# Eight tiles in flight instead of six in the experts phase, with the steps of four engines reordered

## The reference, cut to what matters

```python
def _L0_ffn_ref(x, Wg, W1, W2):
    cap = max(1, T // E)                        # T = 8192 tokens, E = 8 experts
    probs = jax.nn.softmax(xt @ Wg, axis=-1)
    _, top_idx = jax.lax.top_k(probs.T, cap)    # every expert picks its tokens
    ...
    tok2exp = jnp.where(assigned, jnp.argmax(masked, axis=0), jnp.argmax(pT, axis=0))
    weights = jnp.take_along_axis(probs, tok2exp[:, None], axis=1)[:, 0]
    for e in range(E):
        gate = jnp.where(tok2exp == e, weights, 0.0)
        h = jax.nn.gelu(xt @ W1[e], approximate=False) @ W2[e]
        out = out + gate[:, None] * h

xn = _layernorm(x)
s = _L0_attn_ref(xn, ...)                       # the RWKV block
g = _silu(_L0_ffn_ref(xn, Wg, W1, W2))
x = x + s * g
```

## Time and profile before

| | us |
|---|---|
| median of 3 runs | 1236.12 |
| the profiled execution, its own time | 1236.41 |
| its span, first to last instruction | 1234.6 |

### The profile page before, as it was taken

How to read it: one execution, slowest core, us unless ns; L and a number is a source line. 1 busy time by engine, 2 the same in 40 slices (tenths; PEclk the granted TensorE clock), 3 DMA queues, 4 the chain that set the end, 5 groups by cost and what they waited for, 6 DMA issues and landing times. The chain is left out here.

```text
span 1234.6 us, 20795 instructions
## 1 busy us (share of the span) xinstructions
PE 1052.4 (85%) x5440; PEld 836.5 (68%) x5441; DVE 905.4 (73%) x1997; ACT 681.1 (55%) x1233; POOL 371.2 (30%) x403
## 2 busy tenths in 40 slices
PE   5589999999999999999888898998877777777775
PEld 5367877677767767777666676677766666666665
DVE  5899789898898888898986878645555555555554
ACT  2646648568568568567363855744443444433443
POOL 4031321010010010001025537441544454444452
PEclk9789999999999999999988999999999999999999
DMA  9423221011011010010101105351222222222210
GB/s 303 140 86 102 69 85 35 0 53 51 0 51 48 3 51 29 22 51 9 43 14 39 52 1 171 103 185 35 87 66 74 69 70 76 68 72 67 66 50 10
DMA packets 60055, 80.46 MB, mean 65 GB/s; under 512 B 7774, under 2 KB 47327, under 8 KB 60002
## 3 DMA queue, kind: packets, MB, share of 16 engines
q1 hardware_dynamic: 48658, 54.69, 14.0%
q0 software_dynamic: 11360, 25.32, 6.9%
HBM read 65.17 MB, written 26.49 MB: 74 GB/s over the span
## 5 line engine op out<-in xcount | busy, mean ns | idle before, releaser
L916 PE MATMUL psKV<-arena 128*128 128x256 f32 x1024 | 236.1, 385 | 3.4 <-ACT arena L619 1.7
L916 PEld LDWEIGHTS psKV<-arena 128*128 128x128 f32 x1024 | 193.9, 193 | 42.6 <-issue 14.8
L988 PE MATMUL psM<-arena 128*128 128x128 f32 x1152 | 147.1, 281 | 54.6 <-ACT arena L716 48.7
L988 PEld LDWEIGHTS psM<-arena 128*128 128x128 f32 x1152 | 135.7, 193 | 68.8 <-issue 68.8
L709 ACT ACTIVATE arena<-arena,info_t 128x256 f32<-128x256 f32 x72 | 43.1, 600 | 207.5 <-DVE info_t L1486 192.5
L426 POOL TENSOR_SCALAR lnw<-mv 128x4 f32<-128x4 f32 x32 | 8.8, 275 | 485.3 <-DVE mv L1308 485.1
L1557 DVE TENSOR_TENSOR hT_rounded<-arena,hT_rounded 128x512 fp32r<-128x512 f32 x72 | 49.9, 693 | 132.8 <-ACT hT_rounded L728 132.8
L486 POOL DMA_INDIRECT out_dram<-arena,out_idx x72 | 73.2, 1016 | 168.0 <-DVE row_idx L1481 152.1
L1327 DVE SCALAR_TENSOR_TENSOR arena<-arena,vecs 128x512 f32<-128x512 f32 x160 | 108.7, 746 | 0.0
L473 POOL DMA_INDIRECT arena<-xs_rows,row_idx x66 | 100.3, 1519 | 23.1 <-issue 23.1
L886 PE MATMUL psM<-mix_hi,wfk_hi 128*128 128x512 f32 x256 | 103.6, 405 | 2.5 <-ACT mix_hi L608 1.3
(11 more groups left out here) (208 smaller groups left out, 2413.8 us busy)
## 6 DMA issues: line engine op xcount, KB each, us to landing
desk<-in_x SPq DMA_DIRECT2D x16, 512.0 KB, 5.1
arena<-in_x SPq DMA_DIRECT2D x16, 512.0 KB, 4.0
desk<-in_xT SPq DMA_DIRECT2D x16, 512.0 KB, 4.1
xs_rows<-s_ring SPq DMA_DIRECT2D x16, 512.0 KB, 3.2
xs_rows<-in_x SPq DMA_DIRECT2D x16, 512.0 KB, 4.6
desk<-in_W SPq DMA_DIRECT2D x8, 512.0 KB, 8.5
arena<-in_W SPq DMA_DIRECT2D x8, 512.0 KB, 7.5
out_dram<-arena,out_idx POOLq DMA_INDIRECT x72, 2.5
```

The lines of the kernel that those rows point to most:

```text
L916: ins = pe.matmul(psKV[:, j // 2, (j % 2) * C:(j % 2 + 1) * C], kf2[:, h, j * P:(j + 1) * P], wfv[:, h, :], start=(h == 0), stop=(h == HC ...
L988: ins = pe.matmul(psM[:, i % 2, f * P:(f + 1) * P], w1_t[i % 2][:, k, f * P:(f + 1) * P], xnT[i % 2][:, k, :], start=(k == 0), stop=(k == ...
```

## The change

RING goes from 6 to 8, so there are eight buffers for rows and for results, and the steps are written out as 8, 7 passes of 8, and 8. The end of the area for these buffers (`moe_end`) moves behind two more tiles of the first phase. The order inside the steps becomes:

- PE: `mlp_in(t+1)`, `mlp_out(t)`, `turn_x(t+3)`
- ACT: `gelu(t+1)`, `tanh(t)`, `take_xn(t+3)`, `xn(t+4)`
- DVE: `combine(t)`, `take_index(t+8)`, `take_info(t+8)`, `split_h(t+2)`, `mlp_input(t+4)`

What comes ahead of the first step is filled up to match: one `turn_x`, one `take_xn`, one `xn`, one `split_h` and one `mlp_input` more, and eight infos taken at once instead of three.

```diff
-RING = 6
+RING = 8
-        moe_end = at[0]
         mixB_r = part(CH * SEQ)...
         kf2 = part(HC * SEQ)...
+        moe_end = at[0]
...   (ACT)
             def step(t, i, g):
-                if not isinstance(t, int) or t < NT - 3:
-                    xn(t + 3, (i + 3) % RING, g + (i + 3) // RING)
                 if not isinstance(t, int) or t < NT - 1:
                     gelu(t + 1, (i + 1) % RING)
-                if not isinstance(t, int) or t < NT - 2:
-                    take_xn(t + 2, (i + 2) % RING)
                 tanh(t, i)
+                if not isinstance(t, int) or t < NT - 3:
+                    take_xn(t + 3, (i + 3) % RING)
+                if not isinstance(t, int) or t < NT - 4:
+                    xn(t + 4, (i + 4) % RING, g + (i + 4) // RING)
...   (ahead of the steps)
             xn(2, 2, 0)
+            xn(3, 3, 0)
             gelu(0, 0)
+            take_xn(2, 2)
...   (PE)
             def step(t, i, g):
-                if not isinstance(t, int) or t < NT - 2:
-                    turn_x(t + 2, (i + 2) % RING)
                 if not isinstance(t, int) or t < NT - 1:
                     mlp_in(t + 1, (i + 1) % RING)
                 mlp_out(t, i)
+                if not isinstance(t, int) or t < NT - 3:
+                    turn_x(t + 3, (i + 3) % RING)
...   (ahead of the steps)
+            turn_x(2, 2)
             mlp_in(0, 0)
...   (DVE, first_indices)
                 for t in range(RING):
                     take_index(t, t)
-                for t in range(3):
+                for t in range(RING):
                     take_info(t, t)
...   (DVE)
             def step(t, i, g):
-                if not isinstance(t, int) or t < NT - 1:
-                    split_h(t + 1, (i + 1) % RING)
-                if not isinstance(t, int) or t < NT - 3:
-                    mlp_input(t + 3, (i + 3) % RING)
                 ...
                 combine(t, i, g)
                 if not isinstance(t, int) or t < NT - RING:
                     take_index(t + RING, i)
+                    take_info(t + RING, i)
+                if not isinstance(t, int) or t < NT - 2:
+                    split_h(t + 2, (i + 2) % RING)
                 if not isinstance(t, int) or t < NT - 4:
-                    take_info(t + 4, (i + 4) % RING)
+                    mlp_input(t + 4, (i + 4) % RING)
...   (ahead of the steps)
-            take_info(3, 3)
             split_h(0, 0)
             mlp_input(2, 2)
+            split_h(1, 1)
+            mlp_input(3, 3)
```

## The result

The changed kernel takes 1111.32 us, median of four runs (1108.14 to 1112.82), against 1236.08 for the kernel before on the same chip: a ratio of 0.8984 [0.8961, 0.9008]. Two later sets of runs gave 0.8978 [0.8966, 0.8991] and 0.8983 [0.8969, 0.8997]. The forecast was 1124, with a range from 1113: the direction came as predicted, the wait for the infos is gone and PE is the bound, and the gain was 12.7 us larger than forecast. The profiled execution's own time is 1112.54 (span 1109.6).

A forecast was written before the change was run, and what follows sets the result against it. A ring of waits through `take_info`, 5.28 us a tile, was taken as the bound. 870.6 + 67 x 3.6 + 2.5 = 1114.3 for the last `combine` against 1226.77, 112.5 less, so 1124; range 1113 to 1146.

The forecast's parts named there:

- The ring through the info: Experts loop: `xn(t+4)` waits for an info copied only behind `combine(t)`, 5.28 us a tile; infos eight ahead cut it.
- over 3.8 apart: Sign against the forecast: stores in the loop more than 3.8 us apart, where about 3.6 was expected.
- that rival: POOL becomes the bound: 3.80 us a tile gives 1137, with each gather at 1.76, 1151; chance 0.12.
- Register work on PE: Rival: PE's register read before `mlp_out` is exposed, 0.30 a tile, p 3.8 to 3.9, 1144 at the upper end; chance 0.08.
- no instruction was late: Rival: the longer loop body stalls on instruction supply, two stalls of 0.98 a tile, 1255; slower had chance 0.02.
- The longer prologue: Ahead of the loop: extra `turn_x(2)`, 0.2 us, hidden under the first `combine`'s wait for its s rows.
- a moved `combine(0)`: Sign against the forecast: the first tile's `combine` starting elsewhere than 860.5; it was taken to stay at 860.53.
- the period p: Experts loop: time per tile for 67 tiles, taken as 3.6 us; 3.51 to 3.7 gives 1118 to 1131.
- PE's 3.51: Experts loop, PE's stages per tile: `mlp_in` 1.78, `mlp_out` to transposes 1.52, transposes to `mlp_in` 0.21.
- DVE's 3.49: Experts loop, DVE per tile: `split_h` to end of `take_info` 3.35 with all gaps, plus 0.14 hand-over; nearly full.
- the low clock's 1.8 us: Start of experts phase: PE's lower clock after an idle stretch taken to stay adds 1.8, moving `combine(3)` from 868.8 to 870.6.
- The port: Rival: the gather holds DVE's copy 0.81 us, DVE 4.30 a tile, 1171; chance 0.05. The forecast left it out.

The follow-up runs named there:

- `changed_again`: The changed kernel unchanged, timed again on another chip against the kernel before: 1110.34 us, ratio 0.8978.
- `infos_ring8`: The kernel before with infos taken a whole ring ahead and eight buffers, the old order of steps kept: 1151.87 us, ratio 0.9283; again on another chip, 0.9285.
- `dve_more`: The changed kernel with one more 128x256 addition on DVE in each `combine`: 1111.59 us, ratio 0.8986, +1.3 us against the changed kernel.

## Why the prediction was right, and where it was wrong

**Right.** The ring through the info is cut and PE is next. In the loop `xn` doesn't wait, the transposes follow `mlp_out` directly, and PE's steps are 3.42 to 3.48 long. The stores come 3.43 apart on average between 900 and 1055 us, but single ones 2.85 to 3.92, so the sign "over 3.8 apart" holds for their average only. POOL has 0.96 of idle time before the store and is no bound; its step, 0.96 + 1.04 + 0.31 + 1.02, was priced 0.5 too long in that rival, since the gather fell back to 1.02. Register work on PE stayed hidden, and no instruction was late: eight tiles take 8 x 3.42. The longer prologue cost nothing that can be told. The prediction took a moved `combine(0)` as a sign against it, and here it is 1.36 later; but the `memset`s ahead of it already begin 1.31 later (806.66 against 805.35), before anything the change adds, and in `changed_again`, the same kernel, `combine(0)` is at 860.34.

**Wrong: the period p.** The mechanism held and the sum failed in one term, p, which was put at 3.6 us and measured 3.42. "PE's 3.51 at least; with the loop's turn and DVE as full as PE I take 3.6." Whole steps take 3.42, and the 67 tiles from `combine(3)` at 870.52 to `combine(70)` at 1099.23 take 3.414 each, the last two steps having less to do. 67 x 0.186 = 12.5 us of the 12.8 by which the last `combine` came earlier than the 1114.3 forecast (the last tile took 2.31 instead of 2.5). The term is off in two halves:

- 3.51 was not the least. The stages run 1.70, 1.50 and 0.22 (992.72, 994.42, 995.92, 996.14). The forecast had 1.78 for `mlp_in` and 1.52 for `mlp_out`, from start to start. Most of the difference is in the 1.78, which was read where PE had waited 0.83 before `mlp_in`: after a wait that stage runs a little longer, 2.02 as also in `infos_ring8`, beside 1.95 here. Why it does was not tested. Together that is 0.09 a tile, 6 us.
- 0.09 for the turn and for DVE was a margin without a row. The turn costs nothing at a full PE, and DVE has slack, as `dve_more` shows. That is another 6 us. DVE's 3.49 was worked out with its gaps as they are on a waiting engine; they shrink when it falls behind.

**A size that came right by luck.** `combine(3)` was forecast at 870.6 and came at 870.52. In it the low clock's 1.8 us didn't come: the idle stretch that the prediction took to stay is gone. From 860 to 885 us PE is busy for 24.45 of 25 us at a granted clock of 1.00, where it was busy for 19.00 at 0.86 before, and `mlp_in` there took 1.95, not 3.76:

```profile
861.77 1.95 PE L990 MATMUL psM<-arena 128*128 128x128 f32 x16
```

Two things made up for it: tile 0 was 1.36 later, and the three steps took 8.63 where 8.27 was reckoned without the clock.

**Overlooked.** The forecast gave the whole gain to the infos. Alone they bring 91 us of some 127 on a chip of the slower kind. Behind their ring lie two more of nearly one length: `take_xn` behind the GELUs, 3.80 a step, and the six buffers, with which the gather lands too late for `xn`. The prediction checked that the new order and eight tiles close no chain, and so had the right total, but did not see that each of the two was needed. Ratios by what each kernel has:

| infos a ring ahead | new order | eight tiles | ratio |
|---|---|---|---|
| | | x | 0.999 |
| | x | | 1.001 |
| | x | x | 0.999 |
| x | | | 0.927 |
| x | | x | 0.928, 0.929 |
| x | x | | 0.921, 0.923 |
| x | x | x | 0.898 |

The third row and the bottom row are from chips at 1236 to 1237, the others from chips at 1243 to 1245; the changed kernel was not timed on those. With the infos in place the eight tiles alone still bring nothing, and the new order alone 0.005 or 0.006.

**The port.** That DVE's copy isn't held was right: all 70 copies of the changed kernel take 0.68 to 0.74 us. The Trainium skill (SBUF — State Buffer, Who interferes with whom) calls the shared port pair an exclusive lock. Near the end a store that began first, at 1091.91, ran 1.38 us to 1093.29; the copy started inside it, at 1092.47, and ended at 1093.16, in its usual 0.69. The trace disagrees with a lock that the first to start keeps, if what the profile shows as a store's start is when it first needs the port, which was not tested: it is POOL that ends late, 0.13 after the copy, as before with the gathers. Where the copy starts first, POOL is late as well: a store at 908.03, 0.09 behind the start of a copy, took 1.50. But the store at 1095.34 took 1.37 with no copy beside it, so the copy isn't the only thing that makes a store long. These lines are from POOL's and DVE's timeline of the changed kernel.

```profile
907.94 0.69 DVE L1555 COPY arena<-arena 128x1024 f32 x1
908.03 1.50 POOL L486 DMA_INDIRECT out_dram<-arena,out_idx  x1 [1.07 <-DVE row_idx L1484]
...
1091.91 1.38 POOL L486 DMA_INDIRECT out_dram<-arena,out_idx  x1 [2.05 <-DVE arena L1587]
...
1092.47 0.69 DVE L1555 COPY arena<-arena 128x1024 f32 x1
...
1095.34 1.37 POOL L486 DMA_INDIRECT out_dram<-arena,out_idx  x1 [2.05 <-DVE arena L1587]
```

## What to carry to other kernels

When a ring of waits is cut, list the others by length, one step and two steps, on every engine, before giving the gain to one edit: here each of the next two parts was worth nothing by itself, and some 37 and 28 us once the other two were in place (0.928 and 0.921 against 0.898, across chips). The floor of a step is the bound engine's stages read start to start inside a stretch in which it doesn't wait; add no margin for a loop's turn or a second engine without a row that shows one. The gaps of an engine that waits are no measure of what it needs when it is full.

## What the runs showed of the hardware

- An indirect DMA on POOL that DVE's copy of 128x1024 overlaps near its end finishes 0.11 to 0.16 us after the copy, and the copy is not held. Whether a gather or a store is hit follows from the phase of the two: the loop's gathers took 1.55 before and 1.02 after.
- DVE's gap between two independent operations went from 0.92 - 0.69 = 0.23 to none in steps of `dve_more`, where the engine had 0.48 us more to do.
- Chips differ by more than a run's spread: the kernel before takes 1236.1 to 1237.1 on some and 1242.8 to 1244.9 on others. Leaving out the low pass gives 0.887 on the first kind and 0.907 on the second, so a variant must be compared with the changed kernel on one chip. On the second kind one of the first three tiles of the experts phase takes 8.4 to 12.6 us in every trace.
